# First pass of a graph layer: Y and Z of a slice side by side in one bank, 512-column matmuls, two banks per copy

## What is computed

```python
x = x + _L0_gnn_ref(_layernorm(x), W1, b1, W2, b2, [src, dst])
#   agg  = segment_sum(xn[dst], src);  cnt = segment_sum(1, src)
#   mean = agg / max(cnt, 1)
#   xn @ W1.T + b1 + mean @ W2.T + b2
x = x + _L0_ffn_ref(_layernorm(x), ...)     # shared MLP + two of four experts
```

## Time and profile before

| | before |
|---|---|
| median of 3 runs | 3067.03 us |
| lowest to highest | 3060.61 to 3074.59 us |
| the profiled execution | 3059.82 us, its span 3058.3 us |
| TensorE busy | 2936.9 us (96%) |
| VectorE, ScalarE, GpSimd busy | 2441.2, 2096.9, 1717.8 us |

### The profile page before, as it was taken

The page is one execution under the profiler, slowest core; times in us unless marked ns, Lnnn a source line. Parts: engine busy times, 40 slices in busy tenths (PEclk is TensorE's granted clock), DMA queues, the critical chain, the costliest instruction groups (busy, mean ns, idle before and its releaser), DMA issues.

```text
span 3058.3 us, 60717 instructions
## 1 busy us (share of the span) xinstructions
PE 2936.9 (96%) x19417; PEld 2640.6 (86%) x19417; DVE 2441.2 (80%) x7756; ACT 2096.9 (69%) x3807; POOL 1717.8 (56%) x1554
## 2 busy tenths in 40 slices
PE   7999999999949999999999999999999999999998
PEld 7999999999948888888888888888888888888887
DVE  7677677675348888888888888888888888888886
ACT  5665665666637776777777777777777776777775
POOL 1477777777765555555555555555555555555540
PEclk9999999999979999999999999999999999999999
DMA  8778777777654444444444444444444444444441
GB/s 257 226 236 235 222 223 220 237 225 204 159 129 127 120 126 120 127 120 126 122 128 127 128 126 121 125 119 127 126 129 127 123 126 121 125 122 127 119 118 50
DMA packets 271848, 456.82 MB, mean 149 GB/s; under 512 B 146598, under 2 KB 176687, under 8 KB 271526
## 3 DMA queue, kind: packets, MB, share of 16 engines
q1 hardware_dynamic: 203926, 295.51, 36.6%
q10 hardware_dynamic: 30800, 102.42, 10.3%
q0 software_dynamic: 36800, 54.95, 7.4%
HBM read 302.24 MB, written 164.30 MB: 153 GB/s over the span
## 4 chain that ended last, share of the span: by engine, by line
PE 38%; DVE 11%; ACT 11%; issue 8%; DMA 3%; SPq 1%; POOL 1%; DVEq 0%; POOLq 0%; ACTq 0%
PE acc L1241 16%; PE acc L1293 8%; PE acc L1202 7%; ACT h1f L1321 4%; ACT h2f L1334 2%; DVE x_sb L1470 2%; ACT h_hi L1344 2%; DVE l_st L1479 2%; DMA gbc<-gate_d 2%; PE acc L1252 2%; ACT x1n_sb L1379 2%; DVE h_lo L1509 2%; PE acc L1289 1%; PE acc L1222 1%; PE acc L1224 1%
## 5 line engine op out<-in xcount | busy, mean ns | idle before, releaser
L170 POOL DMA_INDIRECT rows<-z_d,tab x500 | 619.0, 1238 | 708.5 <-DVE e_lo L1439 561.7
L1241 PE MATMUL acc<-x1T_hi,wl_hl 128*128 128x500 f32 x2400 | 659.0, 390 | 7.0 <-ACT h1f L1321 7.0
L801 PE MATMUL acc<-w_hl,xT_hi 128*125 128x256 f32 x3200 | 572.1, 283 | 3.9 <-issue 2.9
L182 POOL TENSOR_SCALAR e_oh<-iota_sb,tab 128x250 fp32r<-128x250 f32 (+1 forms) x500 | 428.9, 868 | 241.5 <-PE acc L1224 241.3
L420 POOL DMA_INDIRECT tab_d<-pair,idx x400 | 481.5, 1204 | 136.6 <-issue 130.7
L1241 PEld LDWEIGHTS acc<-x1T_hi,wl_hl 128*128 128x128 f32 x2400 | 445.1, 188 | 91.6 <-ACT h1f L1321 7.4
L1497 DVE TENSOR_TENSOR h_lo<-h1f,h_hi 128x500 fp32r<-128x500 f32 x600 | 397.5, 676 | 111.1 <-ACT h_hi L1328 69.8
L1293 PE MATMUL acc<-wl_hl,h_hi 128*125 128x256 f32 x2400 | 485.2, 282 | 0.0
L801 PEld LDWEIGHTS acc<-w_hl,xT_hi 128*125 128x125 f32 x3200 | 464.5, 187 | 8.3 <-issue 7.6
L1321 ACT ACTIVATE h1f<-acc,bl_sb 128x500 f32<-128x500 f32 x600 | 402.9, 672 | 2.3 <-PE acc L1241 2.1
L1293 PEld LDWEIGHTS acc<-wl_hl,h_hi 128*125 128x125 f32 x2400 | 393.7, 187 | 0.0
(11 more groups left out here) (152 smaller groups left out, 6002.3 us busy)
## 6 DMA issues: line engine op xcount, KB each, us to landing
gbc<-gate_d SPq DMA_DIRECT2D x400, 125.0 KB
xs<-in_x SPq DMA_DIRECT2D x100, 448.0 KB
z_d<-zs ACTq DMA_DIRECT2D x100, 448.0 KB
y_d<-ys ACTq DMA_DIRECT2D x100, 448.0 KB
y_sb<-y_d SPq DMA_DIRECT2D x100, 448.0 KB
x_sb<-in_x SPq DMA_DIRECT2D x100, 448.0 KB
out<-x_sb SPq DMA_DIRECT2D x100, 448.0 KB
e_oh<-code_d SPq DMA_DIRECT2D x25, 488.3 KB
```

The costliest lines, as they stand in the source:

```text
L170: pool.indirect_dma_start(out=rows[g.h][:, q, :], out_offset=None, in_=z_d, in_offset=bass.IndirectOffsetOnAxis(ap=tab[g.h][:, q, 0:1], ax ...
L182: pool.tensor_scalar(e_oh[:, q, w], iota_sb[:, w], tab[g.h][:, q, 1:2].bitcast(F32), None, ALU.is_equal).then_inc(S["e_oh_ready"], 1)
L801: mm = pe.matmul(o, (xT_hi, xT_lo)[a][:, g % 2, f, cols_], w12_hl[:, w, f, wt], start=b == 4 and n == 0, stop=n == 5)
L1241: mm = pe.matmul(bank[L1_BANKS[t]][:, 0:GN], wl1_hl[:, w, f, t * P:(t + 1) * P], (x1T_hi, x1T_lo)[a][:, f, :], start=n == 0, stop=n == 5)
```

## The change

Y and Z of one slice now lie side by side in one bank: slice s has bank 2 + s, Y in its first half and Z in its second. The weights of both are adjacent already, so each product is one matmul of 512 columns. The bias is added to the first half after the two high x high products; the accumulation begins with the first product. The copy of two slices is one instruction over two banks (1024 elements), and it writes `yzs`, one buffer in which the old `ys` and `zs` are halves; its write pattern puts slice and kind back in order. It counts up one semaphore (`a_y`), which both stores wait for, and it waits for the older stores of both.

```diff
-                ys = sb("ys", [SP_, ZB, NS, D], F32, c0)
-                zs = sb("zs", [SP_, ZB, NS, D], F32, c0)
+                yzs = sb("yzs", [SP_, ZB, 2, NS, D], F32, c0)
+                ys, zs = yzs[:, :, 0], yzs[:, :, 1]
...
-                        def half_rows(g, j, to, b, stored, ready):
+                        def half_rows(g, j):
                             act.wait_ge(a_yz, NS * g + 2 * j + 2)
                             if g >= ZB:
-                                act.wait_ge(stored[g % ZB], LOAD * (g // ZB))
-                            act.copy(to[:, g % ZB, 2 * j:2 * j + 2, :],
-                                     bank[b + j][0:SP_, :].rearrange("p (s d) -> p s d", s=2))\
-                               .then_inc(ready, 1)
+                                act.wait_ge(s_y[g % ZB], LOAD * (g // ZB))
+                                act.wait_ge(s_z[g % ZB], LOAD * (g // ZB))
+                            act.copy(yzs[:, g % ZB, :, 2 * j:2 * j + 2, :]
+                                     .rearrange("p k s d -> p s k d"),
+                                     acc[0:SP_, 2 + 2 * j:4 + 2 * j, :]
+                                     .rearrange("p s (k d) -> p s k d", k=2)).then_inc(a_y, 1)
...
-                        def store(g, v, rows_, made, stored):
-                            act.wait_ge(made, 2 * g + 2)
+                        def store(g, v, rows_, stored):
+                            act.wait_ge(a_y, 2 * g + 2)
...
-                            half_rows(g, 0, zs, 4, s_z, a_z)
-                            half_rows(g, 0, ys, 2, s_y, a_y)
+                            half_rows(g, 0)
...
                                 pe.wait_ge(a_y, 2 * (g - 1) + s // 2 + 1)
-                                pe.wait_ge(a_z, 2 * (g - 1) + s // 2 + 1)
...
-                            for b, wt in ((2, slice(0, D)), (4, slice(D, 2 * D))):
-                                o = bank[b + s // 2][0:SP_, (s % 2) * D:(s % 2 + 1) * D]
-                                if b == 2:
-                                    pe.matmul(o, two_ones[:], bias_r[:], start=True, stop=False)
-                                n = 0
-                                for a, w in PARTS:
-                                    for f in range(FT):
-                                        mm = pe.matmul(o, (xT_hi, xT_lo)[a][:, g % 2, f, cols_],
-                                                       w12_hl[:, w, f, wt],
-                                                       start=b == 4 and n == 0, stop=n == 5)
-                                        n += 1
+                            o = bank[2 + s][0:SP_, :]
+                            for a, w in PARTS:
+                                for f in range(FT):
+                                    mm = pe.matmul(o, (xT_hi, xT_lo)[a][:, g % 2, f, cols_],
+                                                   w12_hl[:, w, f, :],
+                                                   start=(a, w, f) == (0, 0, 0),
+                                                   stop=(a, w, f) == (0, 1, FT - 1))
+                                if (a, w) == (0, 0):
+                                    pe.matmul(o[:, 0:D], two_ones[:], bias_r[:], start=False,
+                                              stop=False)
                             mm.then_inc(a_yz, 1)
```

More of the change, by code:

```diff
@@ L305, in build @@
                 a_y = sem("a_y_ready")
-                a_z = sem("a_z_ready")
                 def chunks_of(g):
@@ L757, in _ @@
                             if g:
-                                store(g - 1, z_v, zs, a_z, s_z)
-                                store(g - 1, y_v, ys, a_y, s_y)
+                                store(g - 1, z_v, zs, s_z)
+                                store(g - 1, y_v, ys, s_y)
                             if g + 1 < NG:
@@ L763, in _ @@
                                 norm(g + 2)
-                            half_rows(g, 0, zs, 4, s_z, a_z)
-                            half_rows(g, 0, ys, 2, s_y, a_y)
+                            half_rows(g, 0)
                             if G_WTS <= g < G_WTS + 3:
                                 high_weights(g - G_WTS)
[L768 to L771, removed]
+                            half_rows(g, 1)
+                        store(NG - 1, z_v, zs, s_z)
+                        store(NG - 1, y_v, ys, s_y)
                     @block.tensor
```

## The result

| | before | after |
|---|---|---|
| median | 3066.84 us (4 runs) | 3019.78 us (4 runs) |
| lowest to highest | 3060.61 to 3074.59 us | 3016.59 to 3022.81 us |
| the profiled execution | 3059.82 us | 3019.13 us |
| TensorE: instructions, busy | x19417, 2936.9 us | x17017, 2905.7 us |

The ratio is 0.9845, with an interval of 0.982 to 0.987: 1.5% faster, 47 us. The forecast was 3059 us, "within 0.5%", with a range down to 3038. It was wrong, and even its low edge was 18 us too high.

The account below looks back on a forecast made before the run. The prediction took TensorE to bound the first pass, with ScalarE close behind. Pitch -11, bias -2, fewer instructions -5, later stores +10 and last store +0.4 gave -8 us: 3059 us, range 3038 to 3080.

Parts of the forecast that it names:

- fewer instructions: TensorE's slices: stalls read as late instruction fetches shrink with fewer matmuls and weight loads; 5 us saved (0 to 14).
- the waits for ScalarE: TensorE before its transposes: 19 us of waits in the pass, put down to ScalarE's lateness.
- The pitch: Slice matmuls: 512 columns start 232 ns apart, replacing two of 118.3 ns; 11 us saved.
- Rival 3: TensorE saves nothing: pitch twice that of 256 columns, stalls stay; 3077 us at most, likely 3070; chance 0.13.
- rival 4: 512-column matmuls run much faster per column, GpSimd then limits; 45 us less, 3022 us; chance 0.02.
- Bias and waits: Bias matmul moved behind two large ones; weight-load penalty after semaphore waits kept, 2 us gained (0 to 20).
- The copy: ScalarE's copies out of PSUM: one of 1024 elements replaces two of 512 and lasts 1.02 us.
- Z's later store: ScalarE's queue: Z's store issues 0.37 us later, delaying normalisations that TensorE's transposes need; 10 us added (2 to 20).
- rival 1: First pass: the stores' delay stays hidden and fetch stalls go; 28 us less, 3039 us; chance 0.23.
- The sum: Whole kernel: -11 -2 -5 +10 +0.4 = -8 us, giving 3059 us against the median of the runs shown.
- Rival 2: First pass: ScalarE takes over as the bound; 32 us later at worst, about 3090 us; chance 0.09.

Follow-up runs that it names:

- e2: Changed kernel with 256-column matmuls as before, so only the copies differ from the kernel before: 3055.81 us, ratio 0.9976.
- e1: Kernel before with only the matmuls changed (512 columns, new bank places and bias order), four copies kept: 3008.96 us, ratio 0.9824.
- e3: Changed kernel with two semaphore increments added behind each 512-column matmul, 48 per group: 3068.88 us, ratio 1.0008.
- e4: Kernel before with one semaphore increment added behind each 256-column matmul, 48 per group: 3194.49 us, ratio 1.0417.
- e13: Kernel before itself, unchanged, run and traced in another sitting (D): 3117.31 us, ratio 0.9998.
- e9: Changed kernel run again, in sitting C beside the kernel before: 3023.78 us, ratio 1.0007.
- e11: Changed kernel with the second half's copy split, Z first, so Z's store can start early; sitting C: 3012.61 us, ratio 0.9976.
- e10: The edit of e1 (only the matmuls changed against the kernel before) run again in sitting C: 3011.47 us, ratio 0.9959.
- e8: Kernel before, loading only a quarter of x from group 6 on in the first pass: 3111.64 us, beside 3111.89 for before.
- e6: e1 with Y's stores issued by SyncE instead of ScalarE: 2990.75 us, ratio 0.9618 to the kernel before.
- e12: The edit of e6 run again in sitting C: 2993.29 us, ratio 0.9904 to the kernel before.

## Why the prediction was wrong

**The step that failed is the term "fewer instructions".** It had 5 us, 14 at most. Its mechanism was named rightly: stalls inside slices with the cause "issue" that go with the number of instructions. Its size was not. e2 (small matmuls: 18 clumps), e1 and after (1 and 3), e3 (increments: 50) and e4 tie it to the instructions that TensorE takes per us. In the profiled pair starts that wait for nothing are late by 16 us less, against the 5 forecast; another 10 went at instructions that wait and aren't the first transposes, where a stall and a wait can't be told apart. I had counted the slices' stalls from one row, and never added up the rows of the waits for PEld, 12.8 us for line 801 alone.

**A second step failed: the waits for ScalarE were taken as given.** The forecast read 19 us of them before the transposes and added the later store's price on top. The reading was right, the row "issue" included: 20.3 us of late transposes in before start right behind the normalisation's end. But they don't stay when only the matmuls change. e1 has 5.5 us of them, and all late transposes together fall from 23.4 to 14.8. The forecast had no term for this. They aren't the stalls under another name: e13, with three times the time in clumps, has 13.4 us of them, fewer than before. Why large matmuls make them fewer stays open.

**The pitch: right.** 232 ns forecast, 232 measured, 11 us; by the stretches, 13 with what is left over. Rival 3 falls (237 ns), and so does rival 4: the Trainium skill's sustained gap ("TensorE: Matmul & The Clock Gate", section on the back-to-back issue gap) of 131 ns at 512 columns isn't seen in any stretch of this kernel, where each matmul has its own weight load.

**Bias and waits: wrong by its 2 us.** The first pair behind a wait costs 80 ns more than its median, and the excess summed over the pass is 17.3 us in after and 15.7 before. Nothing was gained.

**The copy: right.** 1008 ns against 1.02 us.

**Z's later store: right in size, +10 forecast, 11 and 12 us measured (e9 against e11 and e10).** But my test for it was unfit. Waits before the transposes of some 30 us were to show it, and under 22 rival 1. They came to 8.4 us from ScalarE and "issue", 18.7 with the 10.3 behind `xT_lo`. That pointed to rival 1, whose claim that the delay stays hidden is refuted by e9 to e11. The test compared with before, whose 19 us were no longer there; beside e1, which has the same matmuls and the early store, the late transposes are 24.5 us instead of 14.8, 9.7 more, and in e9 10.2 more than in e10. The 10.3 us behind `xT_lo` were 1.3 before, but e1 has 8.6, so they are not the store's. The longest of them, 5.5 us, begins at a load of x that lands late; for such loads VectorE waited 22.2 us in after and 10.6 us before.

**The sum.** With the measured terms, -11 for the pitch and -25 for late starts give -36, against -37.8 in the pass. The store's +11 lies within the second: without it, in e1, the late starts fall by 37 us. Rival 1 had the right first half, the stalls go, but valued them at 12 us; its 3039 us is still 19 us above the measured time. Rival 2's sum has a slip: 32 us on the median of 3067 give 3099 us, not 3090.

**A part of it is the sitting, not the change.** Before has 3023, 3064, 3067, 3112 and 3121 us; after has 3020, 3024 and 3043. The ratio goes from 1.001 to 0.974. Where the stalls are few, the change is -11 for the pitch and +11 for the store: zero, as in C. This was not to be had from one trace, but three runs of before 14 us apart and 22 clumps in the trace might have widened the range downwards.

**What stays open** is why TensorE is short of instructions in one sitting and not in another. Sittings A and C were on the same chip (3064 and 3023 us), so it isn't the chip alone. It isn't x's traffic either, as far as the one run e8 tells, and the clumps don't follow the packets on the queue for instructions in any way that I could find: before has 55 in this pass, after 35, and the padded e3 54, as the stalls would have it, but a clump doesn't start at a packet. The granted clock can take a small part at most: over 0 to 850 us it is 0.98 in e13 and 0.99 in before, but 0.97 in after, whose pass is the shortest of the three.

**The best of the kernels** is e6 (and e12), large matmuls with four copies and Y's stores on SyncE. It is at 2990.75 and 2993.29 us in two sittings, where before has 3111.89 and 3022.61, and in the second 30 us under after.

## What to carry to other kernels

Add up the "issue" rows of matmuls and of weight loads, in all places, before giving a price to an edit that removes instructions: where TensorE needs 17 instructions per us (256 columns), it may be fed slower than that for stretches, and larger instructions (9 per us at 512 columns) hide it. But not every "issue" row is a stall: look at what ended just before the start. In front of the transposes it was mostly the normalisation, 52 to 54 ns earlier. And a wait for another engine need not stay when its own engine's instructions change. Merging two copies saves an engine little and delays whoever waited for the first; ask who that is. Run before and after in one sitting, and in several, when the kernel's own time moves by more than the effect.

## What was unexpected of the hardware

- TensorE is fed unevenly. In a clump it resumes about every 0.75 us with some eight instructions (four matmuls with their weight loads); before needs eight per 0.47 us (4 x 118 ns), after eight per 0.93 us (4 x 232 ns), which is slower than the feed.
- The same kernel on the same chip has 3023 us in one sitting and 3064 us in another, and on others 3112 to 3121 us, with runs of one sitting within 20 us of their median. In e13 all but 2 us of the difference lie in the first pass, and most of it in stalls.
- Issuing stores costs the engine that issues them. With Y's two off ScalarE's queue its shortest circle falls from 6.4 us in e1 to 5.4 in e6 (in sitting C, from 6.3 to 6.0), and the kernel by 18 us (3011.47 to 2993.29).
- A late load of x, for which TensorE waits 5.5 us at 212 to 217 us, takes the granted clock of 210 to 220 us to 0.71, in the row of after below (columns as in the earlier trace rows): the clock falls where TensorE was idle. That comes on top of the wait: the seven transposes from 217.53 us take 1.69 us, where eight take 1.07 at 403.48.

```profile
210.00:220.00 10.00, 4.46 (x20) 3.67 (x19) 9.02 (x53) 4.15 (x8) 7.24 (x7) 0.71 0.71 206
```
